# Splitting the next image's first keys into the token buffer, with their two tiles at slots 53 and 54

## The chip, the cores and the metric

One core of a Trainium2 chip runs one program. The metric is the device time in microseconds, the median of the runs. The engines are named as the profile names them: PE (TensorE), DVE (VectorE), ACT (ScalarE), POOL (GpSimd) and SP (SyncE, which here only issues DMAs).

## The reference

The input is x, 8 images of 256 channels by 32 x 32 positions, all float32. Cut to what matters here:

```
xn  = group_norm(xf)                      # 32 groups, xf is (8, 256, 1024)
qkv = w_qkv @ xn + b_qkv                  # 8 heads of 32 channels
w   = softmax(q^T k / sqrt(32))           # 1024 x 1024 per head, over axis 1
x   = xf + w_proj @ (v w) + b_proj
t   = tokens(x)                           # (8, 1024, 256)
t   = t + linear_attention(layer_norm(t)) # elu(qk)+1, rotary, q (k^T v) / z, plus a 3-tap convolution
t   = t + wavelet_mlp(layer_norm(t))      # Haar low band: fc1, gelu, fc2, then back
out = channels(t)
```

The softmax attention needs 64 units per image: 2 groups of 4 heads, times 8 blocks of 128 key rows, times 4 heads. A unit is a score product of 128 x 1024, its row maximum, its exponential with a sum, and a share of the weighted values.

## The kernel before, in words

The program is a software pipeline over the images, written out by hand in `build`. After a prologue come eight bodies, one an image: `first`, six `steady`, `last`; an epilogue finishes image 7. Body i runs the 64 softmax units of image i, one to a slot (slot 0 to slot 63). Between the units of a slot, body i does the work that comes after the softmax for image i-1 (`proj`, `x1T`, `lnT`, `qk`, `kT`, `kv`, `out`, `uT`, `ll`, `fc1`, `fc2`, `rT`), and the work that comes before it: second queries, keys and values of image i (`pq1`, `pk1`, `pv1`), and norm, first queries, keys and values of image i+1 (`gn`, `pq0`, `pk0`, `pv0`). "First" means head group 0, "second" head group 1; the number in a pair such as `("pk0", 1)` is the half of 512 positions.

What an engine does in a slot stands in tables: `PE_STEADY`, `ACT_STEADY`, `DVE_STEADY`, `POOL_STEADY`, and the same for the other kinds of body. Each engine runs its instructions in order. In slot s, PE first makes the scores of unit s+1 and then the tiles that its table gives for s, in the order of the table's entries; ACT makes the exponential of unit s and then its tiles; DVE the maximum of unit s and then its tiles. The scores have two PSUM buffers (`ps_s`), so the scores of unit s+2 wait for the exponential of unit s. The weighted values of four units (`values`, line 623) are due every fourth slot.

All other tiles share two PSUM banks, `work`. `banks` gives them out by turns along the list of tiles, with one exception: `fc2` accumulates over four slots (steps 0 to 3, slots 52, 53, 55 and 56) and holds its bank; a tile between its steps takes the other bank. Before a tile, `claim` makes PE wait until the tile before it in the same bank has been read (`READ`: for a key or query tile that is `lo_done`, for `fc2` it is `band_done`).

A query or key tile is split into two float32r parts: ACT writes the high part (`high_part`, line 875), DVE the low part (`low_part`, line 1015), both reading the PSUM bank. Both go to `hi` and `lo`, which queries and keys share. SP then copies 32-row pieces of them into the operands of the scores: `stack_q` (line 431, 16 DMAs of 128 KB into `q_st`) and `stack_k` (line 449, 16 DMAs of 64 KB for each half of `k_st`). So ACT waits before it overwrites `hi`: the first keys wait for the copies of the first queries (`q_stacked`), and queries wait for the copies of the keys before them (`k_stacked_b`).

SP issues its DMAs in one order; in a steady body: second half of the first keys, second queries, second keys, `half_turn` twice, second half of the second keys, the residual, the next image's first queries, `spread_band` (line 524, waits for `band_done`, which DVE signals when it has read `fc2` at slot 57), the next image's first keys, first half (waits for the low parts of both `pk0` tiles), and the two stores.

The token buffer `t2` holds, one after the other: half-turned queries (rows 0 to 3), the exponentials of the linear attention's elu (`elu_e`, rows 4 to 7, from `qk` at slot 18 on), its output, and the second residual, which the four `rT` transpositions read last, at slot 51. In the first body it holds `fc1_nat`, which the `w1` tiles read at slots 25 and 27.

In the steady bodies PE's tiles from slot 47 on are: rT 0 (47); ll, fc1 0 and 1 (48); fc1 2 to 7, pk0 0 (49); rT 1 (50); rT 2 and 3 (51); fc2 0 (52); fc2 1 (53); fc2 2 (55); fc2 3, pk0 1, pv0 1 (56); and values at 50, 54, 58 and 62. The last body (i = 7) has the same tiles without pq0, pk0 and pv0.

Of the kernel before, what the change touches and what calls it, by code (L numbers as in the profile page):

```python
# [42 lines left out]
for _name, _width in (("bq", 2), ("bk", 2), ("bproj", 2), ("bqk", 4), ("lepe_w", 6), ("lepe_bias", 6),  # L43
# [14 lines left out]
    "pk0": (49, 56), "pv0": (45, 56), "values": (6, 10, 14, 18, 22, 26, 30, 34, 38, 42, 46, 50, 54, 58, 62),  # L58
}
ACT_FIRST = {  # L60
    "copy": (35, 36), "pq1": (12, 13), "pk1": (20, 20), "apply": (41, 42), "pq0": (43, 44), "pk0": (50, 55),
# [4 lines left out]
    "pk0": (51, 57), "pv0": (47, 63),  # L66
# [17 lines left out]
    "pk0": (50, 55),  # L84
# [57 lines left out]
    "turn": (39, 39, 41, 46, 46, 56), "pairs": (62, 62, 63, 63),  # L142
}
# [81 lines left out]
def build(nc, x, wqkv_t, wproj_t, wqk, fc1_t, fc2_t, params, consts, out):  # L225
    with ExitStack() as ctx:
# [59 lines left out]
        elu_e = t2[:, 4:8, :].rearrange("p (a n) c -> p a (n c)", a=2)  # L286
        k_ch = sb("k_ch", [P, 2, HALF])
# [146 lines left out]
        def stack_k(eng, b, g, half, done_units=None):  # L434
            hi_k, lo_k = (hi_first, lo_first) if first_k(b, g) else (hi, lo)
# [68 lines left out]
        def _(sp):  # L504
# [40 lines left out]
            def body(kind, i, post, ahead):  # L545
                if kind != "first":

                    stack_k(sp, i, 0, 1, UNITS * i)
                stack_q(sp, i, 1)
                stack_k(sp, i, 1, 0)  # L550
                if post:
                    for g in range(NG):
                        half_turn(i - 1, g)
                stack_k(sp, i, 1, 1, UNITS * i + PHASE)
                load_residual(i)
                if ahead:
                    stack_q(sp, i + 1, 0)
                if post:
                    spread_band(i - 1)
                if ahead:  # L560
                    stack_k(sp, i + 1, 0, 0)
                if post:
                    for c in range(NC):
                        store(i - 1, c)

            def epilogue():
                for g in range(NG):
                    half_turn(B - 1, g)
                spread_band(B - 1)
                for c in range(NC):  # L570
                    store(B - 1, c)
# [867 lines left out]
```

## Time and profile before

| | us |
|---|---|
| median of 3 runs | 1394.81 (1393.25 to 1395.91) |
| profiled execution, its own time | 1396.55 |
| its span | 1394.8 |
| PE busy | 1227.2 (88%) |
| DVE busy | 992.1 (71%) |
| ACT busy | 879.8 (63%) |
| POOL busy | 467.0 (33%) |
| mean granted clock of PE | 0.949 of 2.4 GHz |

The times of the rows count from the start of the span. A timeline row gives start, duration, engine, line, operation, out<-in, shapes and the number of instructions merged into the row; in brackets stands how long the engine (PEld: the weight load) was idle before it and what ended that. Matmuls overlap in the pipeline, so the durations of neighbouring PE rows add up to somewhat more than the time that passes; the pieces of the chain of waits don't overlap. The page of the profile says that a wait is put down to the event that came last.

### The profile page before, as it was taken

How to read it: one execution, taken by the hardware profiler on the slowest of the kernel's cores; microseconds unless marked ns; L12 is line 12 of the kernel's file. 1: busy time of each engine (PE TensorE's matmuls, PEld its weight loads, DVE VectorE, ACT ScalarE, POOL GpSimd, SP SyncE). 2: the span in 40 equal slices, each digit the busy share in tenths (PEclk: the TensorE clock that was granted, in tenths of full speed). 3: DMA queues.
4: the chain of work that ended last, by engine and by line, in shares of the span. 5: the costliest groups of instructions: out<-in, count | busy, mean ns of one | idle time of the engine just before them, and what ended most of it. 6: DMA issues, size and time to landing. Idle time of an engine off the chain costs nothing.

```text
span 1394.8 us, 21679 instructions
## 1 busy us (share of the span) xinstructions
PE 1227.2 (88%) x7728; PEld 621.5 (45%) x7728; DVE 992.1 (71%) x1607; ACT 879.8 (63%) x1457; POOL 467.0 (33%) x623
## 2 busy tenths in 40 slices
PE   6877799898998999899998989989998989988856
PEld 5333354444445444444445444444545444443433
DVE  2567587867889488866879578975878668885561
ACT  1566568675776668675776668766686757757402
POOL 2001017520285006630275104730175202840450
PEclk9799899999999999999999999999999999989967
DMA  8142315234252224333241243432152242411101
GB/s 265 29 125 79 72 32 136 61 74 106 61 118 76 49 78 122 61 91 91 61 114 55 61 106 72 111 92 59 53 137 66 67 106 62 90 33 31 31 16 46
DMA packets 51354, 111.27 MB, mean 80 GB/s; under 512 B 15504, under 2 KB 15760, under 8 KB 50992
## 3 DMA queue, kind: packets, MB, share of 16 engines
q1 hardware_dynamic: 48576, 100.85, 29.9%
q0 software_dynamic: 2480, 8.78, 2.0%
q8 instruction: 62, 1.02, 0.3%
q14 instruction: 44, 0.36, 0.1%
q10 hardware_dynamic: 192, 0.26, 0.1%
HBM read 21.75 MB, written 8.39 MB: 22 GB/s over the span
## 4 chain that ended last, share of the span: by engine, by line
PE 53%; DVE 28%; ACT 9%; issue 6%; SPq 1%; DMA 1%; POOL 0%; DVEq 0%; POOLq 0%; ACTq 0%
DVE negmax L970 13%; PE ps_s L608 12%; PE ps_o L623 12%; ACT probs L841 7%; PE work L696 6%; PE work L635 4%; PE work L759 4%; PE work L754 3%; DVE tok L1046 3%; PE work L682 3%; DVE ln_st L1035 3%; PE work L647 2%; PE work L736 2%; DVE t L1120 1%; DVE lo L1015 1%
## 5 line engine op out<-in xcount | busy, mean ns | idle before, releaser
L970 DVE TENSOR_REDUCE negmax<-ps_s 128x1 f32<-128x1024 f32 x512 | 620.0, 1215 | 243.2 <-PE ps_s L608 241.6
L841 ACT ACTIVATE probs<-ps_s,negmax 128x1024 f32<-128x1024 f32 x512 | 570.4, 1114 | 321.4 <-DVE negmax L970 316.3
L608 PE MATMUL ps_s<-q_st,k_st 128*128 128x512 f32 x1024 | 408.7, 485 | 78.0 <-ACT probs L841 67.9
L608 PEld LDWEIGHTS ps_s<-q_st,k_st 128*128 128x128 f32 x1024 | 168.8, 195 | 328.3 <-ACT probs L841 198.1
L623 PE MATMUL ps_o<-probs,v_scaled 128*32 128x512 f32 x2048 | 267.6, 643 | 0.5 <-POOL v_scaled L1240 0.5
L1240 POOL TENSOR_TENSOR v_scaled<-v_tok,rsums 128x128 f32<-128x128 f32 x128 | 51.3, 401 | 595.9 <-DVE rsums L976 589.4
L635 PE MATMUL work<-xg,w_qkv 128*128 128x512 f32 x256 | 122.2, 601 | 2.8 <-ACT xg L854 2.8
L623 PEld LDWEIGHTS ps_o<-probs,v_scaled 128*32 128x32 f32 x2048 | 55.9, 113 | 133.7 <-issue 132.1
L696 PE MATMUL work<-ln_ch,w_qk 128*128 128x512 f32 x236 | 113.0, 601 | 2.4 <-DVE k_ch L1146 2.3
L1299 POOL TENSOR_TENSOR x<-x,csum 128x1024 f32<-128x1024 f32 x45 | 106.8, 2372 | 2.6
L841 ACT ACTIVATION_READ_ACCUMULATOR probs<-ps_s,negmax 128x1 f32 x512 | 99.5, 194 | 0.0
L875 ACT ACTIVATE hi<-work,par 128x512 fp32r<-128x512 f32 x62 | 42.3, 683 | 52.9 <-PE work L635 49.4
L635 PEld LDWEIGHTS work<-xg,w_qkv 128*128 128x128 f32 x256 | 47.9, 191 | 49.4 <-issue 39.8
L754 PE MATMUL work<-band,w 128*128 128x512 f32 x118 | 57.1, 615 | 10.0 <-ACT band L913 5.9
L647 PEld LDWEIGHTS work<-w_qkv,xg 128*128 128x128 f32 x512 | 62.5, 196 | 5.5 <-issue 3.3
L1271 POOL TENSOR_TENSOR ln_var<-ln_mv,con 128x2 f32<-128x2 f32 x64 | 12.9, 201 | 150.5 <-DVE ln_mv L1040 150.5
L647 PE MATMUL work<-w_qkv,xg 128*128 128x128 f32 x512 | 62.6, 280 | 0.0
L1015 DVE SCALAR_TENSOR_TENSOR lo<-work,par,hi 128x512 fp32r<-128x512 f32 x62 | 46.2, 745 | 22.6 <-ACT hi L875 22.6
L696 PEld LDWEIGHTS work<-ln_ch,w_qk 128*128 128x128 f32 x236 | 43.1, 190 | 40.6 <-issue 29.1
L759 PE MATMUL work<-shared,w 128*128 128x512 f32 x128 | 60.0, 594 | 0.9 <-ACT shared L916 0.9
L682 PE MATMUL work<-att,w_proj 128*128 128x512 f32 x120 | 56.8, 597 | 0.0
L1296 POOL TENSOR_SCALAR csum<-ln_ch,par 128x1024 f32<-128x1024 f32 x45 | 54.0, 1199 | 0.0
(140 smaller groups left out, 1377.8 us busy)
## 6 DMA issues: line engine op xcount, KB each, us to landing
q_st<-hi SPq DMA_DIRECT2D x128, 128.0 KB, 2.4
q_st<-lo SPq DMA_DIRECT2D x120, 128.0 KB, 2.4
k_st<-hi SPq DMA_DIRECT2D x240, 64.0 KB, 2.0
k_st<-lo SPq DMA_DIRECT2D x240, 64.0 KB, 2.0
x<-in_x SPq DMA_DIRECT2D x8, 1024.0 KB, 5.0
out_x<-ln_ch SPq DMA_DIRECT2D x16, 512.0 KB, 2.9
xg<-in_x POOLq DMA_DIRECT2D x7, 1024.0 KB, 6.4
t<-shared SPq DMA_DIRECT2D x64, 64.0 KB
```

Source lines behind the costliest of these rows:

```text
L608: mm = pe.matmul(ps_s[s % 2][:, half * HALF:half * HALF + HALF], k_st[:, h, j * P:j * P + P], q_st[g][:, h, half * HALF:half * HALF + HALF ...
L623: mm = pe.matmul(ps_o[D * h:D * h + D, cols], v_scaled[:, j % 2, D * h:D * h + D], probs[:, j % 2, h, cols], start=(j == 0), stop=(j == NB ...
L635: mm = pe.matmul(bank(tile)[:, :], w_qkv[:, c, col:col + P], xg[:, c, half * HALF:half * HALF + HALF], start=(c == 0), stop=(c == NC - 1))
L647: mm = pe.matmul(bank(tile)[:, P * n:P * n + P], xg[:, c, P * nb:P * nb + P], w_qkv[:, c, col:col + P], start=(c == 0), stop=(c == NC - 1))
L682: mm = pe.matmul(ps[:, :], w_proj[:, g, P * c:P * c + P], att[:, g, half * HALF:half * HALF + HALF], start=(g == 0), stop=(g == 1))
L696: mm = pe.matmul(ps[:, :], w_qk[:, c, col:col + P], ln_ch[:, c, 1 + half * HALF:1 + half * HALF + HALF], start=(c == 0), stop=(c == NC - 1))
L754: pe.matmul(ps[:, :], w1[:, P * n:P * n + P], band[:, :], start=True, stop=True)\
L759: mm = pe.matmul(ps[:, :], w2[:, k, :], hid[:, k, :], start=(k == 0), stop=(k == 7))
L841: act.activation(probs[:, j % 2, h, :], ps_s[s % 2][:, :], ACT.Exp, bias=negmax[:, s % 4:s % 4 + 1], accum_out=sums[:, j % 2, h:h + 1]).th ...
L970: dve.tensor_reduce(negmax[:, s % 4:s % 4 + 1], ps_s[s % 2][:, :], AX_X, ALU.max, negate=True)\
L1015: dve.scalar_tensor_tensor(out=lo_to[:, cols], in0=bank(tile)[:, :], scalar=param("bk" if is_k else "bq", g), in1=hi_from[:, cols].bitcast ...
L1299: pool.tensor_tensor(x1[:, c, :], x1[:, c, :], lepe_product, ALU.add).then_inc(lepe_step, 1)
```

## The change

The two first-key tiles get buffers of their own in `t2`, which is free of its old content after the last `rT`. PE makes both tiles later or earlier than before: `pk0` goes from slots (49, 56) to (53, 54), ACT's part from (50, 55) to (53, 54), DVE's from (51, 57) to (54, 55), in the first and the steady bodies. ACT's high part of the first keys no longer waits for the copies of the first queries, but for the last `rT` of the image in `t2` (in the first body for `w1`). The second queries no longer wait for the copies of the first keys, but for those of the first queries. The first elu exponential waits for the late copies of the first keys. SP's order is now a table, and the same order as before; its names and the tile `late_up`, which no table uses, change nothing that is issued.

```
 PE_STEADY / PE_FIRST
-    "pk0": (49, 56)
+    "pk0": (53, 54)
 ACT_STEADY / ACT_FIRST
-    "pk0": (50, 55)
+    "pk0": (53, 54)
 DVE_STEADY / DVE_FIRST
-    "pk0": (51, 57)
+    "pk0": (54, 55)

+SP_ORDER = {
...
+    "steady": ("late_keys0", "queries1", "keys1", "half_turn0", "half_turn1", "late_keys1",
+               "residual", "queries0", "spread", "keys0", "store"),
...
+        hi_keys, lo_keys = (t2[:, 4 * n:4 * n + 4, :].rearrange("p n c -> p (n c)").bitcast(F32R) for n in range(2))
...
+        def key_parts(b, g):
+            if first_k(b, g):
+                return hi_first, lo_first
+            return (hi_keys, lo_keys) if g == 0 else (hi, lo)
...
         def stack_k(eng, b, g, half, done_units=None):
-            hi_k, lo_k = (hi_first, lo_first) if first_k(b, g) else (hi, lo)
+            hi_k, lo_k = key_parts(b, g)
...
             def high_part(i, tile):
...
-                hi_to = hi_first if is_k and first_k(b, g) else hi
-                if not (isinstance(done, int) and done == 0):
-
-                    if is_k:
+                hi_to = key_parts(b, g)[0] if is_k else hi
+                if done > 0:
+                    if is_k and g == 0:
+
+                        if b == 1:
+                            act.wait_ge(made["w1"], 2)
+                        else:
+                            act.wait_ge(made["rT"], 4 * (b - 1))
+                    elif is_k:
                         act.wait_ge(q_stacked, 16 * DMA * (done + 1) - LACK)
-                    else:
+                    elif g == 0:
                         act.wait_ge(k_stacked_b, 16 * DMA * done)
+                    elif b > 0:
+                        act.wait_ge(q_stacked, 16 * DMA * done - LACK)
...
                 elif name == "qk":
                     if n >= 2:
...
+                    elif n == 0 and b + 1 < B:
+                        act.wait_ge(k_stacked_b, 16 * DMA * (2 * b + 3))
```

## Rows read from the trace of the kernel before

**Rows 1.** The page: busy time of each engine.
```profile
PE 1227.2 (88%) x7728; PEld 621.5 (45%) x7728; DVE 992.1 (71%) x1607; ACT 879.8 (63%) x1457; POOL 467.0 (33%) x623
```

**Rows 2.** Chain of waits, steady body 2: start us, us, what.
```profile
456.12 5.79 PE work L754 x12
...
477.20 0.47 PE ps_s L608 x2
...
479.39 1.73 PE work L635 x4
...
486.72 0.68 PE ps_s L608 x2
```

**Rows 3.** Timeline of PE, steady body 2, slots 52 to 63, and slot 0 after.
```profile
468.41 1.92 PE L759 MATMUL work<-shared,w 128*128 128x512 f32 x4
...
484.13 0.73 PE L608 MATMUL ps_s<-q_st,k_st 128*128 128x512 f32 x2 [0.36 <-ACT probs L841]
...
490.00 0.73 PE L608 MATMUL ps_s<-q_st,k_st 128*128 128x512 f32 x2 [1.75 <-ACT probs L841]
...
491.85 3.21 PE L623 MATMUL ps_o<-probs,v_scaled 128*32 128x512 f32 x16
494.99 1.53 PE L608 MATMUL ps_s<-q_st,k_st 128*128 128x512 f32 x4
496.36 3.73 PE L647 MATMUL work<-w_qkv,xg 128*128 128x128 f32 x32
```

**Rows 4.** Timeline of PE, last body (no pk0), slots 49 and 52.
```profile
1257.23 5.79 PE L754 MATMUL work<-band,w 128*128 128x512 f32 x12 [0.59 <-ACT shared L916]
...
1268.86 1.88 PE L759 MATMUL work<-shared,w 128*128 128x512 f32 x4
```

**Rows 5.** Timeline of ACT, steady body 2, and the first elu of body 3.
```profile
465.05 0.68 ACT L875 ACTIVATE hi<-work,par 128x512 fp32r<-128x512 f32 x1
...
481.20 0.69 ACT L875 ACTIVATE hi<-work,par 128x512 fp32r<-128x512 f32 x1 [5.66 <-PE work L635]
...
485.12 1.11 ACT L841 ACTIVATE probs<-ps_s,negmax 128x1024 f32<-128x1024 f32 x1 [1.04 <-DVE negmax L970]
...
488.74 1.11 ACT L841 ACTIVATE probs<-ps_s,negmax 128x1024 f32<-128x1024 f32 x1 [1.28 <-DVE negmax L970]
...
536.60 0.68 ACT L905 ACTIVATE t<-work,par_elu 128x512 f32<-128x512 f32 x1
```

**Rows 6.** Timeline of DVE, steady body 2: fc2 read, low part of pk0 1.
```profile
479.43 0.75 DVE L1127 SCALAR_TENSOR_TENSOR band<-work,par,band 128x512 f32<-128x512 f32 x1 [0.49 <-PE work L759]
481.92 0.75 DVE L1015 SCALAR_TENSOR_TENSOR lo<-work,par,hi 128x512 fp32r<-128x512 f32 x1 [1.75 <-ACT hi L875]
```

**Rows 7.** Timeline of SP's issues, end of steady body 2.
```profile
480.20 2.42 SPq L524 DMA_DIRECT2D csum<-band  x4
...
492.16 0.59 SPq L449 DMA_DIRECT2D k_st<-lo  x1
```

**Rows 8.** DMA issues, 478 to 500 us: KB each, median us to landing.
```profile
k_st<-lo SPq DMA_DIRECT2D x12, 64.0 KB, 2.0
```

**Rows 9.** Timeline of SP, then PE, end of steady body 3.
```profile
653.55 0.59 SPq L449 DMA_DIRECT2D k_st<-lo  x1
...
655.76 1.39 PE L608 MATMUL ps_s<-q_st,k_st 128*128 128x512 f32 x4
```

**Rows 10.** Timeline of PE, then ACT, first body, slots 49 to 51.
```profile
141.84 3.04 PE L635 MATMUL work<-xg,w_qkv 128*128 128x512 f32 x4
144.32 1.03 PE L608 MATMUL ps_s<-q_st,k_st 128*128 128x512 f32 x2
...
147.74 0.69 ACT L875 ACTIVATE hi<-work,par 128x512 fp32r<-128x512 f32 x1 [3.13 <-DMA q_st<-lo]
```

**Rows 11.** Stretches: busy us (count) by engine, granted clock, DMA share, GB/s.
```profile
461.91:483.04 21.13, 20.98 (x99) 10.89 (x99) 11.00 (x12) 12.97 (x22) 0.80 (x2) 1.00 0.08 18
491.80:495.10 3.30, 3.30 (x18) 0.65 (x17) 3.17 (x4) 2.34 (x4) 0.00 (x0) 0.58 0.63 214
```

More of the change, by code:

```diff
@@ L57 @@
     "w1": (25, 27), "pq1": (11, 12), "pv1": (0, 0), "pk1": (19, 20), "gn": (39,), "pq0": (43, 44),
-    "pk0": (49, 56), "pv0": (45, 56), "values": (6, 10, 14, 18, 22, 26, 30, 34, 38, 42, 46, 50, 54, 58, 62),
+    "pk0": (53, 54), "pv0": (45, 56), "values": (6, 10, 14, 18, 22, 26, 30, 34, 38, 42, 46, 50, 54, 58, 62),
 }
 ACT_FIRST = {
-    "copy": (35, 36), "pq1": (12, 13), "pk1": (20, 20), "apply": (41, 42), "pq0": (43, 44), "pk0": (50, 55),
+    "copy": (35, 36), "pq1": (12, 13), "pk1": (20, 20), "apply": (41, 42), "pq0": (43, 44), "pk0": (53, 54),
 }
@@ L65 @@
     "pq1": (13, 14), "pk1": (21, 21), "stats": (28, 33, 34, 37), "moments": (38,), "gn": (40,), "pq0": (44, 45),
-    "pk0": (51, 57), "pv0": (47, 63),
+    "pk0": (54, 55), "pv0": (47, 63),
 }
@@ L83 @@
     "fc1": (49, 49, 49, 49, 49, 49, 49, 49), "pq1": (12, 13), "pk1": (20, 20), "apply": (41, 42), "pq0": (43, 44),
-    "pk0": (50, 55),
+    "pk0": (53, 54),
 }
@@ L142 @@
     "turn": (39, 39, 41, 46, 46, 56), "pairs": (62, 62, 63, 63),
+}
+SP_ORDER = {
+    "first": ("late_keys0", "queries1", "keys1", "late_keys1", "residual", "queries0", "keys0"),
+    "steady": ("late_keys0", "queries1", "keys1", "half_turn0", "half_turn1", "late_keys1",
+               "residual", "queries0", "spread", "keys0", "store"),
+    "last": ("late_keys0", "queries1", "keys1", "half_turn0", "half_turn1", "late_keys1",
+               "residual", "spread", "store"),
+    "epilogue": ("half_turn0", "half_turn1", "spread", "store"),
 }
@@ L543, in prologue, with issue, body @@
                 stack_k(sp, 0, 0, 1)
[L545 to L556, printed above, removed]
+            def issue(i, name):
+                if name == "late_keys0":
+                    if i > 0:
+                        stack_k(sp, i, 0, 1, UNITS * i)
+                elif name == "queries1":
+                    stack_q(sp, i, 1)
+                elif name == "keys1":
+                    stack_k(sp, i, 1, 0)
+                elif name == "late_keys1":
+                    stack_k(sp, i, 1, 1, UNITS * i + PHASE)
+                elif name == "half_turn0":
+                    half_turn(i - 1, 0)
+                elif name == "half_turn1":
+                    half_turn(i - 1, 1)
+                elif name == "residual":
+                    load_residual(i)
+                elif name == "queries0":
                     stack_q(sp, i + 1, 0)
-                if post:
+                elif name == "keys0":
+                    stack_k(sp, i + 1, 0, 0)
+                elif name == "spread":
                     spread_band(i - 1)
-                if ahead:
-                    stack_k(sp, i + 1, 0, 0)
-                if post:
+                elif name == "store":
                     for c in range(NC):
                         store(i - 1, c)
-            def epilogue():
[L567 to L571, printed above, removed]
+                elif i >= 2:
+                    for c in range(NC):
+                        store(i - 2, c)
+            def body(kind, i, post, ahead):
+                for name in SP_ORDER[kind]:
+                    issue(i, name)
+            def epilogue():
+                for name in SP_ORDER["epilogue"]:
+                    issue(B, name)
                 sp.wait_ge(stored, NC * DMA * B)
@@ L1013, in low_part @@
                 cols = slice(half * HALF, half * HALF + HALF)
-                hi_from, lo_to = (hi_first, lo_first) if is_k and first_k(b, g) else (hi, lo)
+                hi_from, lo_to = key_parts(b, g) if is_k else (hi, lo)
                 dve.scalar_tensor_tensor(out=lo_to[:, cols], in0=bank(tile)[:, :],
@@ L1060, in post_tile @@
                 name, n = tile
-                b = image_of(i, tile)
-                ps = None if name == "up" else bank(tile)
+                b = i - 2 if name == "late_up" else i - 1
+                if b < 0:
+                    return
+                ps = None if name in ("up", "late_up") else bank(tile)
                 if name == "proj":
```

2 lines of the change are left out of this document (1 added, 1 removed), and 4 rows, old and new, of tables (DVE_STEADY, PE_STEADY).

## The prediction

> **What bounds the kernel now.** I read the page first: PE is busy 88% of the span, DVE 71%, ACT 63% [rows 1]. Busy shares are means over unlike stages, so I then followed the chain through the end of a steady body, where all the edits lie, and laid the timelines of the four engines beside it. The six steady bodies repeat (the scores after the last values start at 494.99 and at 655.76, 160.77 us apart [rows 3, 9]); I work on body 2 and check at body 3.
>
> From the end of the last fc1 (461.91 us) to the scores of unit 58 (483.04) PE is busy 20.98 of 21.13 us at the full clock [rows 11], and the chain of waits runs through PE into pk0 1 [rows 2]. The eye is drawn to ACT: before the high part of pk0 1 it stands idle for 5.66 us [rows 5], since its slot (55) comes before PE's (56). But that idle time ends on PE, and all it costs PE afterwards is a wait of 0.36 us before the scores of unit 59 [rows 3]. After unit 58 the bound changes: PE has little to do, the clock falls to 1.2 GHz for the last values (granted 0.58 over that stretch [rows 11]; these take 3.21 us [rows 3]), and the body ends with two things close together: PE comes free at 494.99 [rows 3], and the last of the 16 copies of the next keys is issued at 492.16 and lands 2.0 us later, at 494.2 [rows 7, 8]. In body 3 it is 653.55 + 2.0 = 655.55 against 655.76 [rows 9]. So the key copies are hidden by 0.8 us here and 0.2 us there, no more.
>
> **The change part by part.** No instruction is added or removed that takes engine time: the same two tiles of 1.73 us on PE [rows 2], two high parts, two low parts and 32 copies. What counts is what each stands behind.
>
> *Waits edited.* In the steady bodies the high part of pk0 0 did not wait for the query copies: there is no idle time before it [rows 5], so that wait's removal gives nothing there. The second queries are due only at slot 12, long after the copies that they waited for. The new wait for the last rT is met at slot 53, two slots after it. The new wait of the first elu is on 16 copies that SP issues behind the first 16 and the stores; at 0.59 us each [rows 7] they are out some 10 us into body 3, and the elu starts at 536.60 [rows 5], 42 us into it: 30 us of cover; were it gone, the exponentials behind the elu on ACT would stand. SP's order is what it was. I cost all these at nothing.
>
> *Pk0 0 leaves slot 49.* The last body is the same stretch without that tile. From the start of fc1 2 to fc2 0 it takes 1268.86 - 1257.23 = 11.63 us [rows 4], body 2 takes 468.41 - 456.12 = 12.29 us [rows 2, 3]. So the tile's 1.73 us cost only 0.66 there: the rest lay beside the last gelus, ACT's table load and the exponential behind them. Gain 0.66, while 1.07 us of cover is given up.
>
> *Both tiles go to slots 53 and 54.* PE is full there, so they cost 2 x 1.73 = 3.46 us ahead of fc2 3.
>
> *Their bank.* fc2 holds one of the two banks from slot 52 to 56, so both tiles get the other one, and pk0 1 must wait for the low part of pk0 0. How long, the old pk0 1 shows: PE done at 479.39 + 1.73 = 481.12 [rows 2], high part at 481.20 [rows 5], low part 481.92 to 482.67 [rows 6], so 1.55 us. PE has the scores of unit 55 to do meanwhile, 0.47 us after a tile like these [rows 2], so it stands 1.08 us. Behind the claim in PE's queue are the values of slot 54 and all scores. Bounds: 0.87 (scores at the 0.68 us they take after values [rows 2]) to 1.55 (nothing beside it). fc2 3, and with it the read of fc2 that sets `band_done`, is late by 3.46 + 1.08 - 0.66 = 3.88 us.
>
> *The bank of pv0 1.* It takes the bank that fc2 leaves, before as now. The DVE read of fc2 ends at 480.18, 0.79 us after fc2 3 [rows 2, 6]. Before, pk0 1 stood between and hid it; now nothing does: PE waits 0.79 us. pv0 1 began at 481.12 and now begins at 479.39 + 3.88 + 0.79 = 484.06, that is 2.94 us late (pk0 1 no longer stands behind fc2 3, so this is less than 3.88 + 0.79), and the scores of unit 58 with it.
>
> *After slot 58.* ACT is no longer held, so the 0.36 us wait goes, and the values of slot 58 are late by at most 2.6. The scores of unit 60 wait for the exponential of unit 58, which began at 485.12 and now begins at 488.06. Scores follow the start of the exponential that frees their buffer by 1.26 us (488.74 to 490.00 [rows 3, 5]), so they come at 489.32; before, PE reached them at 486.72, after its values [rows 2]. From there the loop of scores, maximum and exponential runs as before: PE reaches the end of the body 2.6 us late.
>
> *The copies.* SP spreads the band at 480.20, at once on `band_done`, and is done with it at 482.62 [rows 7]; the keys' low part (482.67) is ready at the same moment. Now the low parts are early but `band_done` is 3.88 late, and the keys stand behind it in SP's queue. Last landing: 492.16 + 3.88 + 2.0 = 498.04, against PE at 494.99 + 2.6 = 497.59. The copies now end last: body 2 is 3.05 us longer, body 3 655.55 + 3.88 - 655.76 = 3.67. I take the mean, 3.36. Steady bodies: 6 x 3.36 = +20.2 us.
>
> *First body.* Here ACT did wait for the query copies, 3.13 us, and the scores of unit 51 stood 2.48 us behind pk0 0 (141.84 to 144.32) [rows 10]. At most both go, 5.6 us; at 53 and 54 one tile (1.73) and the wait for its split (1.08) come back into a loop that isn't bound by PE. I take -2.8, bounds 0 and -5.6.
>
> Sum: 20.2 - 2.8 = +17.4 us. The profiled execution took 1396.55 us, so 1413.9 in its measure; it lay 1.7 above the median, from which the forecast is 1394.81 + 17.4 = 1412.2 us.
>
> A rule weighed: the Trainium skill (Perfetto Trace Analysis, Matmuls) wants independent matmul groups to rotate through different PSUM banks, so that reading one overlaps the next. The change goes against it: two tiles in one bank. By the rule the 1.08 us of every steady body is the fault of the placing, and a free second bank would bring the sum to about +11.
>
> **The rivals.**
>
> 1. *The copies are not the end* (they land earlier than I have it, and PE's own path decides): 2.6 a body, 6 x 2.6 - 2.8 = +12.8, 1407.6 us. For it: 0.8 us of slack in body 2. Against: 0.2 in body 3.
>
> 2. *The clock follows the new idle time.* At the end of a body PE now waits some 0.5 to 1 us more, and there are new gaps. If the low stretch falls on the 32 value matmuls at the start of the next body (3.73 us at the full clock [rows 3]) and covers half of them, 1.8 us a body is added: 17.4 + 11 = +28, 1423 us. For it: the clock fell after just such a wait [rows 3, 11]. Against: in the old trace one stretch a body is low, and it may land where PE waits anyway. The Trainium skill (TensorE: Matmul & The Clock Gate, HAM oscillation) has this as a rule: bursts parted by waits start at the lower clock each time. By it this rival would be the forecast; the granted clock of rows 11 bears out one such burst in a body, not two.
>
> 3. *ACT's idle 5.66 us is the bound, and the kernel gets faster.* With both key tiles early, ACT runs its exponentials ahead, the waits of pk0 1 and pv0 1 are hidden behind scores already fed, and the low parts let the copies go early. Then each steady body keeps the 0.66 and the 0.36 and loses nothing: 6 x -1.0 - 2.8 = -9, 1386 us. It decides if PE had under 1 us of work per slot in slots 53 to 56. Against it: 20.98 of 21.13 us busy, and the copies stand behind `band_done`.
>
> 4. *It comes out even:* the waits are half as long and the first body gives its full 5.6 us; or the tiles are placed so that nothing on the path moves. About 1395 us.
>
> **How the numbers follow.** Forecast 0.53; rival 1 0.17; rival 2 0.15; rival 3 0.10; rival 4 0.05. The low end: the smallest steady loss that the rows allow, 2.94 less the 0.36 that ACT gives back and less 0.21 for the lower bound of the bank wait, 2.37 a body, and the full gain of the first body: 14.2 - 5.6 = +8.6, 1403.4, less the 1.6 us by which the lowest run lies under the median, 1402. The high end: 3.67 a body, and rival 2 on top: 22 - 2.8 + 11 = +30, 1425. Rival 3 is left outside. About 0.2% (2.8 us) is what can be told from no change here. Slower 0.85, within it 0.05, faster 0.10.
>
> **What would show it.** Steady bodies longer by 3 to 4 us, all of it behind the last gelu; PE idle about 1.1 us before pk0 1 with DVE's low part as releaser, and 0.8 us before pv0 1 with the fc2 read; ACT's 5.66 us wait gone, with short ones before both high parts; the spread issued 3.9 us later after fc1, the key copies right behind it, and the scores of the next image waiting for `k_st`; the first body shorter by some 3 us with no DMA wait on ACT. Wrong would be: no wait on PE before these tiles, or key copies issued ahead of the band.

## The result, and the profile of the changed kernel

The changed kernel takes 1415.05 us (median of 4 runs, 1408.35 to 1420.81) beside 1395.36 us for the kernel before on the same chip (1393.25 to 1397.97). The ratio is 1.0137, interval 1.0091 to 1.0182: 12.7 to 25.4 us slower. The forecast was 1412.2 us, range 1402 to 1425. The profiled execution is the lowest of the four, 1408.35 us. Two runs of the experiments below, 1651.85 us of b_keys_first and 2933.88 us of g_act_56, lie far above the others of their kernels and are left out of every number.

The page, to be held against [rows 1]:

```profile
span 1406.6 us, 21684 instructions
PE 1219.5 (87%) x7728; PEld 618.0 (44%) x7728; DVE 993.8 (71%) x1607; ACT 880.4 (63%) x1457; POOL 467.0 (33%) x623
```

PE is busy 7.7 us less than before, in a span that is 11.8 us longer. So the loss is waiting. To find where, divide the span at the row of twelve fc1 matmuls, of body 1 and of the last body:

| stretch | before | changed | difference |
|---|---|---|---|
| start to fc1 of body 1 | 296.33 | 290.05 | -6.28 |
| six steady bodies | 960.90 | 981.01 | +20.11 (3.35 each) |
| last fc1 to the end | 137.57 | 135.54 | -2.03 |

Only the middle row repeats. A second profile of the same changed kernel (k_after_again) has 296.23, 981.55 and 137.52 us: the gains of the first and the last row are not there.

The steady part, as the view of stretches has it, changed kernel (stretch, its length, then busy us and count of PE, PEld, DVE, ACT, POOL, granted clock, DMA share, GB/s):

```profile
290.05:1271.06 981.01, 883.98 (x5722) 444.38 (x5723) 729.45 (x1184) 654.82 (x1089) 351.61 (x452) 0.98 0.32 78
```

and the kernel before:

```profile
296.33:1257.23 960.90, 883.24 (x5722) 444.41 (x5722) 729.45 (x1184) 653.83 (x1089) 351.63 (x452) 0.98 0.33 80
```

The work of every engine is the same within 1 us, at the same clock; 19.4 of the 20.11 us are idle time of PE. All of it lies between fc1 and the end of the body: from the value matmuls of slot 0 to the next row of twelve a body takes 119.89 us on the mean before and 119.92 after. Now the timeline of PE in body 2 of the changed kernel, to be read beside [rows 2, 3] (start us, us, engine, line, operation, tiles; in brackets the idle time before it and what ended it):

```profile
454.24 5.79 PE L779 MATMUL work<-band,w 128*128 128x512 f32 x12 [0.59 <-ACT shared L950]
...
465.87 1.88 PE L784 MATMUL work<-shared,w 128*128 128x512 f32 x4
...
469.76 1.88 PE L660 MATMUL work<-xg,w_qkv 128*128 128x512 f32 x4
...
473.26 1.98 PE L660 MATMUL work<-xg,w_qkv 128*128 128x512 f32 x4 [1.16 <-DVE t L1049]
...
482.49 2.05 PE L672 MATMUL work<-w_qkv,xg 128*128 128x128 f32 x16 [0.84 <-DVE band L1163]
...
487.62 0.73 PE L633 MATMUL ps_s<-q_st,k_st 128*128 128x512 f32 x2 [0.29 <-ACT probs L866]
...
490.97 0.73 PE L633 MATMUL ps_s<-q_st,k_st 128*128 128x512 f32 x2 [1.48 <-ACT probs L866]
492.83 3.62 PE L648 MATMUL ps_o<-probs,v_scaled 128*32 128x512 f32 x16
496.52 1.17 PE L633 MATMUL ps_s<-q_st,k_st 128*128 128x512 f32 x4
```

Two waits are new. The first, 1.16 us on DVE's low part, stands before the second key tile, in the same bank as the first (469.76 and 473.26). The second, 0.84 us on DVE's read of fc2, stands before the value tile in slot 56. The weighted values of slot 62, the last ones, still run at the low clock, as in [rows 3, 11]. ACT, same body:

```profile
471.74 0.69 ACT L907 ACTIVATE t<-work,par 128x512 fp32r<-128x512 f32 x1 [3.15 <-PE work L660]
...
475.34 0.69 ACT L907 ACTIVATE t<-work,par 128x512 fp32r<-128x512 f32 x1 [1.82 <-PE work L660]
```

ACT's 5.66 us of idle time [rows 5] have become 3.15 and 1.82, together 4.97. And SP's queue:

```profile
482.47 2.42 SPq L540 DMA_DIRECT2D csum<-band  x4
484.93 10.10 SPq L465 DMA_DIRECT2D k_st<-t  x16
```

Before, the spread was issued 24.08 us after the twelve fc1 matmuls began [rows 2, 7], now 28.23 us: 4.15 late. The 16 key copies follow at once and take 10.1 us to issue here. Does their landing end the body? In body 2 it can't be told, since the slow value matmuls last until about the same time (492.83 + 3.62 = 496.45, scores at 496.52). In body 5 they ran at the full clock, and the chain of waits says it outright (start us, us, what):

```profile
985.49 2.00 DMA k_st<-t
987.49 0.09 issue
987.58 1.17 PE ps_s L633 x4
```

The timeline of PE for the same place:

```profile
983.87 1.92 PE L648 MATMUL ps_o<-probs,v_scaled 128*32 128x512 f32 x16
987.58 1.17 PE L633 MATMUL ps_s<-q_st,k_st 128*128 128x512 f32 x4 [1.78 <-DMA k_st<-t]
```

A PE that was through 1.7 us earlier (values of 1.92 us instead of 3.62) gains nothing: the scores of the next image come where the last copy lets them. The landing times in the trace say the same of bodies 1 to 5: the scores start 0.09 us after the last of the 16 copies has landed. Only in body 6 does PE end last, 0.48 us after the landing. In the kernel before it was PE in all six bodies, and the last copy had landed 1.16, 0.84, 0.22, 0.75, 0.91 and 0.81 us ahead of the scores, 0.78 on the mean. Last, the views of waits over the six bodies (us in total, times, longest). The kernel before:

```profile
ACT hi L875 <- PE work L635: 40.3, 15, 5.7
```

The changed kernel, in which `t` is the keys' high part alone and `hi` the other ones:

```profile
ACT t L907 <- PE work L660: 30.1, 12, 3.4
...
ACT hi L907 <- PE work L660: 7.5, 10, 0.9
...
PE work L660 <- DVE t L1049: 7.2, 6, 1.4
...
PE work L672 <- DVE band L1163: 5.1, 6, 0.8
...
PE ps_s L633 <- DMA k_st<-t: 1.8, 1, 1.8
```

The two new waits of PE come once in each of six bodies, 7.2 and 5.1 us in total. Of ACT's 40.3 us before, 34.0 (six times 5.66) stood before the second key tile; the keys' waits are 30.1 us now, only 4 less, and none of that is found in the time.

### The profile page after: what moved, and what is told of

It reads as the page before. It is cut to its first block, busy times and chain, and to the rows that moved or that the text cites. A ratio compares the mean times of both kernels' runs of the same rounds, so it can differ in the third digit from the quotient of the medians.

```text
span 1406.6 us, 21684 instructions
## 1 busy us (share of the span) xinstructions
PE 1219.5 (87%) x7728; PEld 618.0 (44%) x7728; DVE 993.8 (71%) x1607; ACT 880.4 (63%) x1457; POOL 467.0 (33%) x623
## 3 DMA queue, kind: packets, MB, share of 16 engines
q8 instruction: 62, 1.02, 0.3%
## 4 chain that ended last, share of the span: by engine, by line
PE 51%; DVE 29%; ACT 10%; issue 6%; SPq 1%; DMA 1%; POOL 0%; DVEq 0%; POOLq 0%; ACTq 0%
DVE negmax L1004 14%; PE ps_s L633 11%; PE ps_o L648 10%; ACT probs L866 7%; PE work L721 6%; PE work L660 4%; PE work L784 4%; PE work L779 3%; DVE ln_st L1069 3%; PE work L672 3%; DVE tok L1080 3%; PE work L707 3%; DVE t L1156 1%; DVE lo L1049 1%; PE work L761 1%
## 5 line engine op out<-in xcount | busy, mean ns | idle before, releaser
L648 PE MATMUL ps_o<-probs,v_scaled 128*32 128x512 f32 x2048 | 264.2, 636 | 0.2 <-POOL v_scaled L1276 0.2
L660 PE MATMUL work<-xg,w_qkv 128*128 128x512 f32 x256 | 121.0, 597 | 10.1 <-DVE t L1049 7.2
L721 PEld LDWEIGHTS work<-ln_ch,w_qk 128*128 128x128 f32 x236 | 43.0, 190 | 41.6 <-issue 29.3
L950 ACT ACTIVATE shared<-work,par 128x512 f32<-128x512 f32 x59 | 39.9, 687 | 14.7 <-PE work L779 14.6
L1310 POOL TENSOR_TENSOR ln_rs<-ln_var,con 128x2 f32<-128x2 f32 x64 | 44.9, 702 | 5.0
```

What stands on the lines that cost most here:

```text
L648: mm = pe.matmul(ps_o[D * h:D * h + D, cols], v_scaled[:, j % 2, D * h:D * h + D], probs[:, j % 2, h, cols], start=(j == 0), stop=(j == NB ...
L660: mm = pe.matmul(bank(tile)[:, :], w_qkv[:, c, col:col + P], xg[:, c, half * HALF:half * HALF + HALF], start=(c == 0), stop=(c == NC - 1))
L721: mm = pe.matmul(ps[:, :], w_qk[:, c, col:col + P], ln_ch[:, c, 1 + half * HALF:1 + half * HALF + HALF], start=(c == 0), stop=(c == NC - 1))
```

## The experiments

Eleven runs; "ratio" is against the kernel before on the same chip. Their profiles are compared by positions in a steady body, in us after its first fc1 tile, from the timelines. The first four columns give the lowest of the six bodies; where the clock is low at the first fc1 tile, all that follows stands some 0.8 us later (up to 1.1 in i_after_fill). The last two give the lowest and highest start of the value matmuls of the next slot 0, and the mean length of the six bodies:

| kernel | value tile (slot 56) starts | spread issued | first key copy | values of slot 62 start | value matmuls of next slot 0 | mean body |
|---|---|---|---|---|---|---|
| before | 27.84 | 27.10 | 29.60 | 38.75 | 43.26 to 43.31 | 160.15 |
| changed | 31.26 | 31.24 | 33.70 | 41.60 | 46.29 to 47.89 | 163.50 |
| a_old_buffers | 31.26 | 31.24 | 33.70 | 41.60 | 46.29 to 47.23 | 163.76 |
| b_keys_first | 31.26 | 35.88 | 25.61 | 41.60 | 45.72 to 48.19 | 163.55 |
| c_second_55 | 30.24 | 30.21 | 32.67 | 40.58 | 45.26 to 46.80 | 162.51 |
| d_first_only | 27.82 | 27.09 | 29.58 | 38.74 | 42.15 to 43.58 | 159.72 |
| e_second_54 | 28.83 | 28.81 | 31.27 | 39.16 | 43.86 to 44.31 | 160.21 |
| f_values_57 | 31.27 | 31.24 | 33.71 | 40.77 | 46.35 to 48.32 | 163.88 |
| g_act_56 | 27.83 | 27.09 | 29.59 | 38.06 | 42.37 to 44.69 | 159.68 |
| h_fill | 27.82 | 27.09 | 29.58 | 38.73 | 42.13 to 43.44 | 159.03 |
| i_after_fill | 31.27 | 31.24 | 33.70 | 41.60 | 46.29 to 49.50 | 163.90 |
| j_fill_56 | 27.82 | 27.08 | 29.58 | 38.06 | 42.15 to 43.33 | 160.02 |
| k_after_again | 31.27 | 31.24 | 33.71 | 41.60 | 46.30 to 47.40 | 163.59 |

The last positions of the kernel before rest on slow last values in every body (3.20 to 3.49 us). Where they ran at the full clock with its slots it is 42.15 (one body of d_first_only) and 42.13 (h_fill).

The 16 key copies take the same time to issue in most bodies, but not in all: 10.05 to 10.10 us in bodies 1, 2, 5 and 6 of the kernels before and changed, 10.3 in body 4, 10.85 and 10.88 in body 3. In body 3 of the experiments it is up to 11.70 us (f_values_57), with single copies that land after up to 3.46 us instead of 2.0. What delays them there is not shown.

**Slots or buffers: a_old_buffers.** The kernel before with the new slots alone; buffers and semaphores stay.

```
-    "pk0": (49, 56),      PE, first and steady
+    "pk0": (53, 54),
-    "pk0": (50, 55),      ACT
+    "pk0": (53, 54),
-    "pk0": (51, 57),      DVE
+    "pk0": (54, 55),
```

> The kernel before with only the slots changed to those of the changed kernel (PE 53 and 54, ACT 53 and 54, DVE 54 and 55, first and steady bodies); buffers hi and lo and all waits as before. My theory (the slots alone make the loss, the buffers do nothing at these slots): steady bodies of 163.4 us on the mean, as in the changed kernel (981.01 us for six), the first body 6 us shorter than before, total within 3 us of the changed kernel's runs, about +12 to +20 us against before. Rival (the loss or the first body's gain comes from the buffers and waits in the token buffer): steady bodies at 160.2, total near 1395, or the 3.1 us query-copy wait of the first body is back before the high part of pk0 0.

1412.63 us (1409.85 to 1416.97), ratio 1.0108 (1.0071 to 1.0144); steady bodies of 163.76 us, the lowest positions equal to the changed kernel's to 0.01. The slots alone make the loss. The expected shorter first body did not come: fc1 of body 1 starts at 296.26 us, as before (296.33).

**SP's order: b_keys_first.** The changed kernel with the keys ahead of the spread in SP's steady order.

```
-               "residual", "queries0", "spread", "keys0", "store"),
+               "residual", "queries0", "keys0", "spread", "store"),
```

> The changed kernel with one swap in SP's order of the steady bodies: the next image's first keys before the spread of the band. Theory (key copies and PE's own path end within 0.1 us of each other, the first set by band_done): the key copies start about 8 us earlier, the scores of the next image no longer stand behind them, and a steady body falls from +3.4 to about +2.9 over before (PE's own path), so 3 us less in all than the changed kernel; the spread is issued some 5 us later than now, after 16 copies, and the last step of the body (up, slots 61 and 63) may wait for it by up to 2 us without harm to the scores. Rival (the copies in truth set the whole of the loss): steady bodies return to 160.2, total below 1395. Rival 2 (the copies don't matter at all): no change.

1410.84 us over 3 runs (1409.63 to 1417.81), ratio 1.0115 (1.0072 to 1.0159), bodies of 163.55 us: the expected gain of 0.5 us a body, 3 us in all, is not seen in the bodies, and the intervals are too wide to tell it in the time. That is the outcome of the second rival, but not for its reason. The key copies went out 8 us earlier and no score waited for them. But the spread now stands behind 16 of them in the queue, and the timeline of DVE in body 2 shows who needs it:

```profile
492.36 1.23 DVE L1170 SCALAR_TENSOR_TENSOR ln_ch<-csum,ln_ch 128x1024 f32<-128x1024 f32 x1 [1.27 <-DMA csum<-band]
```

In the view of waits over the kernel (the changed kernel has this wait once, 4.4 us in the last body):

```profile
DVE ln_ch L1170 <- DMA csum<-band: 10.0, 7, 4.4
```

At the low clock nothing is gained even without that: in body 2 the values of slot 62 start at 41.6 and take 3.5 us as in the changed kernel, and with the copies out of the way PE's own path ends the body at the same point (46.27 to 46.29). At the full clock PE is through early, but DVE's wait has made the maxima late, then the exponentials, and PE waits for these, body 4:

```profile
820.07 1.92 PE L648 MATMUL ps_o<-probs,v_scaled 128*32 128x512 f32 x16
822.58 0.70 PE L633 MATMUL ps_s<-q_st,k_st 128*128 128x512 f32 x2 [0.59 <-ACT probs L866]
```

In the two bodies at the full clock, 4 and 6, the value matmuls of the next slot 0 come 0.57 and 0.14 us earlier than 46.29 (45.72 and 46.15), no more. So three things end within about half a microsecond of each other: the copies, PE with slow values, and, once the order is turned, the spread.

**The bank wait of the second key tile: c_second_55.** In the changed kernel that tile one slot later, fc2 2 between the two.

```
-    "pk0": (53, 54),      PE and ACT
+    "pk0": (53, 55),
-    "pk0": (54, 55),      DVE
+    "pk0": (54, 56),
```

> The changed kernel with the second key tile a slot later: PE (53, 55), ACT (53, 55), DVE (54, 56). The values of slot 54, scores 56 and fc2 2 now lie between the two tiles in the one bank. Theory (the bank wait of pk0 1 costs 1.1 us and 0.25 for the restart): PE has no wait before pk0 1, fc2 3 ends about 1.2 us earlier after fc1, a steady body is 1.2 to 1.4 us shorter than the changed kernel's (163.5 to about 162.2), total about -8 us against the changed kernel. Rival (that wait is covered by the later waits of the softmax loop): steady bodies stay at 163.4.

1411.14 us (1406.51 to 1411.8), ratio 1.0097 (1.0064 to 1.0129); bodies of 162.51 us, 1.0 shorter; 1.2 to 1.4 and a total of -8 us were expected, and the total is 4 us below the changed kernel's, with intervals that overlap. The wait before the key tile is gone, and the spread is issued 1.03 earlier in every body, which is the firmer measure. Part of the 1.16 comes back before the value tile, in the timeline of PE of c_second_55:

```profile
476.20 1.88 PE L660 MATMUL work<-xg,w_qkv 128*128 128x512 f32 x4
478.38 1.88 PE L784 MATMUL work<-shared,w 128*128 128x512 f32 x4
481.50 2.05 PE L672 MATMUL work<-w_qkv,xg 128*128 128x128 f32 x16 [1.24 <-DVE band L1163]
```

**The first body alone: d_first_only.** New slots in the first body, the old ones in the steady bodies.

> The kernel before with the new slots in the first body alone (PE 53 and 54, ACT 53 and 54, DVE 54 and 55), steady bodies, buffers and waits as before. Theory (the first body gains since ACT no longer stands for the query copies, and no fc2 holds a bank or fills PE there): fc1 of body 1 starts 6 us earlier than before (290 instead of 296.3), steady bodies 160.2, total about 1389, 5 to 7 us faster than before. Rival (the first body's gain needs the new buffers, or is the clock's luck in one execution): 0 to -2 us.

1390.51 us over 10 runs (1386.99 to 1398.35), ratio 0.9968 (0.9944 to 0.9992): -4.5 us, between -7.8 and -1.1. Old buffers do as well; the query copies, for which ACT waited 3.13 us [rows 10], have simply landed by slot 53. But in the profile fc1 of body 1 starts at 296.45 us, not at the expected 290 (before: 296.33), so the trace does not show where the gain lies.

**Only the second tile moved: e_second_54.** d_first_only with it in slot 54 and the first in slot 49 as before.

```
-    "pk0": (49, 56),      PE, steady
+    "pk0": (49, 54),
```

> The kernel of d_first_only (before, new slots in the first body) with only the second key tile moved in the steady bodies: PE (49, 54), ACT (50, 54), DVE (51, 55); the first tile stays beside the gelus at slot 49. Theory (what costs is the tile's time ahead of fc2 3, the two bank waits and the copies behind band_done): no wait before pk0 1, fc2 3 ends 1.73 us later after fc1 than before, PE waits 0.8 before pv0 1, the spread is issued 1.7 us later, the last key copy lands at 42.8 us after the first fc1 instead of 41.1, and a steady body grows by 0.6 (clock low at the last values) to 1.7 us (clock full), so 4 to 10 us over d_first_only, about 1396. Rival (ACT's 5.66 us of idle time before the high part of pk0 1 is what costs, and only the pairing of the two tiles spoils its removal): steady bodies shorter than 160.2 us, total under 1388.

1395.79 us over 10 runs (1388.23 to 1403.17), ratio 1.0007 (0.9975 to 1.0038), bodies of 160.21 us. PE has no wait before the key tile, 0.84 us before the value tile, and the spread is 1.7 late; the next image begins 0.6 later than before. Of the 3 us by which the next image is late in the changed kernel, the one tile ahead of fc2 costs 0.6 beyond the cover of the slow values, the other tile and the bank wait between them the rest. The mean body shows less of it (160.21 beside 160.15), since its six bodies have less low clock, 30.7 us beside 44.4.

**The wait of the value tile: f_values_57.** The changed kernel with PE's `"pv0": (45, 57)`.

> The changed kernel with the second half of the next image's first values (pv0 1) on PE at slot 57 instead of 56, so that the scores of unit 58 stand between fc2 3 and the tile that waits for fc2's bank. Theory (the copies behind band_done end the body): PE's wait before pv0 1 falls from 0.84 to about 0.35 us, band_done and the key copies stay where they are, and the value matmuls of the next slot 0 still start 46.3 us after the first fc1; steady bodies 163.5 us, no change of the total beyond 2 us. Rival (PE's own path ends the body): steady bodies 0.5 to 0.8 us shorter, total 3 to 5 us less.

1417.5 us (1414.73 to 1419.7), ratio 1.0142 (1.0091 to 1.0194), bodies of 163.88 us. The wait before the value tile is 0.38 us and PE's own path some 0.5 earlier (values of slot 62 at 40.8 to 41.5), spread and copies are not, and the next image begins no earlier. The 0.84 us wait costs nothing behind these copies.

**ACT's idle time in the old kernel: g_act_56.** d_first_only with ACT's high part one slot later, behind the exponential instead of ahead of it.

```
-    "pk0": (50, 55),      ACT, steady
+    "pk0": (50, 56),
```

> The kernel of d_first_only with ACT's high part of pk0 1 at slot 56 instead of 55 in the steady bodies, where PE makes the tile; nothing else moves. It takes away most of ACT's idle 5.66 us alone. Theory (that idle time costs PE only the 0.36 us before the scores of unit 59): the exponential of unit 56 runs some 4 us earlier, the wait of 5.66 us shrinks to about 4 (it is still PE's tile that ends it), and a steady body is shorter by 0 to 0.4 us, total within 2 us of d_first_only. Rival (ACT's stall is the bound): a steady body shorter by 1 us or more.

1390.70 us over 9 runs (1385.32 to 1398.73), ratio 0.9957 (0.993 to 0.9984), no different from d_first_only (1390.51) in time. The timeline of ACT in body 2 shows the wait 2.5 us smaller than [rows 5]:

```profile
476.24 0.69 ACT L875 ACTIVATE hi<-work,par 128x512 fp32r<-128x512 f32 x1 [3.15 <-PE work L635]
```

The values of slot 58 come 1.06 earlier, those of slot 62 0.68 earlier, the next image 0.7 earlier at the low clock. That is all that 2.5 us less of idle time brings, more than the 0.36 us expected and less than the rival's 1 us.

**The clock at the end of the body: h_fill and i_after_fill.** Two matmuls that nobody reads, into a bank that is free, in PE's idle time of slots 60 and 61: h_fill is d_first_only with them, i_after_fill the changed kernel with them. Nothing of the computation changes.

```
+ if ahead and s in (60, 61):
+     pe.wait_ge(lo_done, 8 * (i + 1) + 4)
+     pe.matmul(bank(("pk0", 1))[:, 0:(HALF if s == 60 else P)], const("ident"),
+               const("cos_ch")[:, 0:(HALF if s == 60 else P)], start=True, stop=True)
```

> The kernel of d_first_only with two extra matmuls a body whose result nobody reads (one of 512 and one of 128 columns, after the tiles of slots 60 and 61), in the time in which PE stands idle before the scores of units 62 and 63. Theory (the clock falls to 1.2 GHz over the last values because PE stood idle before; in the kernel before this, not the copies, ends the body): the values of slot 62 take 1.9 instead of 3.2 to 3.5 us, the next body starts 42.2 instead of 43.3 us after the first fc1, where the copies end it; steady bodies 159.1 to 159.3 us, total some 5 to 7 us under d_first_only, about 1384. Rival (the clock falls anyway, or the fill delays the scores): steady bodies 160.3 or longer. For the changed kernel this says how much of its loss hides behind the low clock.

> The changed kernel with the two extra matmuls of h_fill (512 columns after slot 60, 128 after slot 61, result unread). Theory (in the changed kernel the key copies end the body whether the clock is low or full at the last values): the values of slot 62 take 1.9 us instead of 3.6, the value matmuls of the next slot 0 still start at 46.3 us after the first fc1, steady bodies 163.3 to 163.6 us, so the fill, which took 10 us off the kernel without the moved tiles, takes 0 to 3 us here (only what it saves at other low stretches), total 1408 to 1415. Rival (clock and PE path still decide in the changed kernel): 6 us or more less than it.

h_fill: 1386.63 us over 7 runs (1381.3 to 1391.53), ratio 0.9914 (0.9883 to 0.9944), 12 us below the kernel before, bodies of 159.03 us. Below d_first_only it lies 3.9 us by the medians and 7.5 by the ratios, since the kernel before was at 1396.77 us beside the one and 1398.70 beside the other. The timeline of PE, h_fill, body 2:

```profile
480.81 1.02 PE L822 MATMUL work<-con 128*128 128x512 f32 x2
...
483.27 0.38 PE L822 MATMUL work<-con 128*128 128x128 f32 x2
...
484.57 1.92 PE L623 MATMUL ps_o<-probs,v_scaled 128*32 128x512 f32 x16
486.96 1.18 PE L608 MATMUL ps_s<-q_st,k_st 128*128 128x512 f32 x4 [0.47 <-DMA k_st<-lo]
```

The last values take 1.92 us instead of 3.21 [rows 3], in every body, and then the copies end it, 1.1 us earlier than the slow values did in bodies 1, 5 and 6. In body 3, where the copies take 11.36 us to issue, nothing is gained. i_after_fill: 1414.62 us (1409.93 to 1420.04), ratio 1.0118 (1.0078 to 1.0157), nothing against the changed kernel. Its timeline of PE:

```profile
500.77 1.92 PE L648 MATMUL ps_o<-probs,v_scaled 128*32 128x512 f32 x16
...
504.47 1.17 PE L633 MATMUL ps_s<-q_st,k_st 128*128 128x512 f32 x4 [1.77 <-DMA k_st<-t]
```

Here too the values run at the full clock in every body, and the scores come where they came: 1.77 us of waiting for the copies has taken the place of slow matmuls. These two kernels have the same clock over the last values in every body and differ in the steady slots (and the buffers, which a_old_buffers shows to be worth nothing). Their lowest positions at the next slot 0 are 42.13 and 46.29, 4.16 apart, and the spread is issued 4.15 apart (27.09 and 31.24). That is the cleanest measure of the cause: where nothing else disturbs a body, it grows by what the spread is late. The mean bodies are 4.87 apart (159.03 and 163.90), single bodies 2.97 to 7.11; low stretches fall differently in the two profiles, and in body 3 of i_after_fill the four copies of the spread took 3.98 us to issue instead of 2.42. The runs do not separate these.

**Together, and once more: j_fill_56 and k_after_again.** j_fill_56 is h_fill with g's slot for ACT; k_after_again the changed kernel itself.

> h_fill and g_act_56 together: before, new slots in the first body, ACT's high part of pk0 1 at slot 56 and the two extra matmuls. Theory (with the clock full, the copies of the next keys end the body at 42.15 us after the first fc1, and an earlier PE gains nothing more): steady bodies as in h_fill, total within 2 us of it, about 1386. Rival (ACT's stall still counts): 3 us or more less than h_fill.

> The changed kernel itself once more, for a second profile and more times. Its runs so far lie between 1408 and 1421 us, the profiled one at 1408. Theory (the spread comes from where the low stretches of the clock fall, not from the copies): steady bodies again in the range of 162.4 to 164.5 us with key copies always first issued 2.45 us after the spread, a median near 1414, and in bodies without a low stretch the value matmuls start 46.3 us after the first fc1. Rival (copies vary): the time from the spread to the start of the value matmuls differs between bodies at the same clock.

j_fill_56: 1388.22 us (1382.43 to 1394.18), ratio 0.9926 (0.9898 to 0.9954). PE is 0.67 earlier at the values of slot 62 (38.06), but the copies let the next image begin at 42.15, as in h_fill (42.13): no gain. Its bodies are 160.02 us on the mean, not as in h_fill; the profile is that of its slowest run, and the value matmuls of slot 0 were slow in two of its bodies. k_after_again: 1418.47 us (1413.33 to 1423.14), ratio 1.0146 (1.01 to 1.0192), bodies of 163.59 us. Its rival has a part in it: the first key copy always goes out 2.47 us after the spread, but the copies take 10.09 to 11.19 us to issue, and in body 4, at the full clock, the next image begins at 46.54, 0.24 later than in body 6.

## Why the prediction was right

By its own steps, body 2, times taken from the first fc1 tile:

- **Waits edited, at nothing.** Confirmed: a_old_buffers, without those edits, has the changed kernel's lowest positions.
- **Pk0 0 leaves slot 49, gain 0.66.** fc2 0 comes 11.63 us after the twelve fc1 matmuls (465.87 - 454.24), before 12.29: 0.66.
- **Two tiles at 1.73, bank wait 1.08.** The wait is 1.16, and the chain gives 1.98 us for the tile behind it, 0.25 more than for one that did not wait. c_second_55 shows the wait itself: 1.0 us a body.
- **`band_done` late by 3.88.** Measured 4.14: 0.26 above, a little less than the longer wait (0.08) and that longer tile (0.25) make together.
- **The bank of pv0 1, 0.79 and 2.94 late.** Measured 0.84, and 3.25 late against the 481.12 us from which the step counted. It does not matter for the end (f_values_57).
- **PE 2.6 late at the end.** 2.85 in bodies 2 and 5 (the values of slot 62 start at 38.75 and 41.60), 3.1 to 3.4 in the others. Rival 1, in which this path alone sets the end, does not hold: while the copies stand behind `band_done`, a faster PE gains nothing (body 5, f_values_57, i_after_fill). But at the low clock its path ends level with the copies in body 2 (b_keys_first), since the slow values took 3.62 us here instead of 3.21, and in body 6 it ends 0.48 us after them. The prediction had the copies 0.45 us later than PE.
- **The copies set the end, +3.36 a body, +20.2 in all.** Measured 3.35 and 20.11. The mechanism is right, but an agreement this close is luck: two errors cancel. `band_done` is 0.26 later than the sum had it. Against that, the mean over bodies 2 and 3 gave body 3, where the copies had only 0.22 us of cover, half of the weight; the cover over all six bodies is 0.78 us, which with the prediction's 3.88 would have given 3.10 a body. How much the cover is worth also depends on the clock: at the low clock the slow values hide 1.1 us of the loss (43.28 to 46.29 is 3.0); at the full clock it is 4.16.
- **First body, -2.8.** This reading was wrong. The 2.48 us by which the scores of unit 51 stood behind pk0 0 were no wait of PE: the tile itself took 3.04 us because the clock was low there (1.88 in the changed kernel's profile, below). ACT's 3.13 us wait is gone, but from the value matmuls of slot 45 to slot 0 of body 1 PE stood idle for 7.82 us before and for 7.29 (changed), 7.65 (d_first_only) and 7.66 us (k_after_again) with the new slots: 0.2 to 0.5 us less. The whole stretch took 42.67, 37.47, 40.96 and 41.14 us, with granted clocks of 0.84, 0.95, 0.88 and 0.88, so nearly all of the difference is where the low stretches of the clock fell. The runs of d_first_only do show a gain (-4.5 us, interval -7.8 to -1.1), and whether the slots make it by moving the low stretches stays open; k_after_again, with the same first body as the changed kernel, has none up to fc1 of body 1 (296.23 us beside 296.33).

Timeline of PE of the changed kernel, first body, the two key tiles, to set against the 3.04 us tile in [rows 10]:

```profile
149.97 1.88 PE L660 MATMUL work<-xg,w_qkv 128*128 128x512 f32 x4
...
152.15 1.88 PE L660 MATMUL work<-xg,w_qkv 128*128 128x512 f32 x4
```

The high part between them waited 1.40 us, for PE, and not for a DMA:

```profile
151.94 0.69 ACT L907 ACTIVATE t<-work,par 128x512 fp32r<-128x512 f32 x1 [1.40 <-PE work L660]
```

**The sum and the profiled execution.** The profile shows +11.8, the medians +19.7, a gap of 7.9. The records have 143.3 us of low clock in the old profiled execution and 120.4 in the changed one; 22.9 us at half speed are some 11 us of PE's work, if all of it lay on the path (an estimate). That is enough for the gap, and the runs go the same way: granted clock 0.958 at 1408.35 us, 0.950 at 1420.81. The profile of k_after_again, with 139.8 us of low clock, is 20.5 us longer than the old one (1415.3 beside 1394.8), 20.65 of it in the six steady bodies. So one profiled execution beside one other could have misled by half the effect; the six steady bodies, with the same mean clock on both sides, did not.

**Rival 2, the clock.** The prediction counted one low stretch a body. The records show two in most bodies of the kernel before, one over the last values and one some 100 us later, and one to three in the bodies of the changed kernel; over the six bodies they are 44.4 us in each, a mean clock of 0.98 on both sides. The value matmuls of slot 0, which this rival made slow, run in 3.73 us in all six bodies of the changed kernel. Bodies 3 and 4 begin their next image 1.6 and 1.0 us later than bodies 2 and 5: 0.8 of each is a low clock at the first fc1 tile, 0.8 and 0.2 are the copies, issued in 10.88 and 10.31 us instead of 10.09. So it was no steady cost. But what the rival feared does happen elsewhere: in six bodies of other kernels (two of f_values_57 and of j_fill_56, one of g_act_56 and of i_after_fill) these matmuls took 4.4 to 5.1 us, each time after PE had waited 1.9 to 3.6 us for the copies; in body 4 of k_after_again, after 2.00 us, they took 3.73. The Trainium skill (TensorE: Matmul & The Clock Gate, HAM oscillation) describes bursts that start at the lower clock each time, and these are shorter than the DMA waits between them; that is not the case here, so the prediction went too far where it said that by it this rival would be the forecast. The new waits of 1.16 and 0.84 us, in a stretch where PE was otherwise busy, were not followed by a low clock. The low clock over the last values follows waits of 0.29, 0.40, 1.48 and 0.46 us in body 2, but in body 5 the same waits are followed by values of 1.92 us.

**Rival 3, ACT's idle time.** Not the bound, and the prediction's own size was off too: it booked 0.36 us for the 5.66, and g_act_56, which takes 2.5 us of them away, shows 0.7 (values of slot 62) to 1.06 (values of slot 58) on PE and nothing in the time. The change itself took only 4 us of that wait away over the six bodies (34.0 to 30.1), and the same edit put 4.14 us in front of `band_done`.

**Rival 4, even.** The steady bodies are 20 us longer and the ratio's interval lies above 1, so this one is out.

**The rule weighed.** The Trainium skill (Perfetto Trace Analysis, Matmuls) wants independent matmul groups to rotate through different banks. What two tiles in one bank cost is measured by c_second_55: 1.0 us a body. So a free bank would leave some +14 of the steady +20 (an estimate, 20.1 less six times 1.0; no run has it). Most of what delays `band_done`, 3.46 less 0.66 of 4.14 us, is not the bank but the place ahead of fc2.

**What stays open.** Which low stretches a given execution gets; what delays the copies of body 3; and what the -4.5 us of d_first_only are made of. The changed kernel's runs lie 12 us apart, and no edit here separates the causes outside slots 60 to 63.

## What to carry to other kernels

Before moving work, list what stands behind it in program order and which signals it delays, and then which transfers wait in an order-bound queue behind such a signal: here 4.15 us in front of one semaphore became 4.16 us at the end of an undisturbed body (h_fill and i_after_fill), and 3.35 us on the mean beside the kernel before, through copies that had 0.2 to 1.2 us of cover. Idle time of an engine that waits for the bound engine is not a reserve: taking 2.5 of its 5.66 us away was worth 0.7 us on PE and nothing in the time. Before booking a gap between two starts as a wait, look at the granted clock over it: 2.48 us in the first body were one tile at half speed. Where two paths end together, moving either alone gains almost nothing (b_keys_first at the low clock, f_values_57, i_after_fill and j_fill_56); take the one that ends last, and then look at what is next.

## What the runs showed of the hardware

- With two unread matmuls, 1.02 and 0.38 us long, in idle time of PE the values that follow ran at the upper clock: 1.92 us in all six steady bodies of h_fill, of i_after_fill and of j_fill_56, in place of 3.2 to 3.6 in most bodies without them. In a kernel that is 87% busy, 1.4 us of useless work a body gave, with the first body's slots, 12 us of 1398; the part of the two matmuls is 4 us by the medians and 7.5 by the ratios. Behind later copies (i_after_fill) it gave nothing that the intervals show.
- The same program ran at mean clocks of 0.950 to 0.958 in successive executions, 1408 to 1421 us. The differences of d, e, g, h and j stand on 7 to 10 runs each.
- The 16 copies of 64 KB took 10.05 to 10.12 us to issue behind the spread in most bodies and 10.3 to 11.7 in bodies 3 and 4; ahead of it (b_keys_first) 10.0 to 11.0. PE working or waiting beside them made no difference (10.10 and 10.09 us in bodies 2 and 5 of the changed kernel); what moved their end in most bodies is when they start.
